# Softmax denominators by a streamed sum in four column groups, and context transposes moved ahead of the turned reciprocals

## The chip, the cores and the metric

The kernel runs on one core of one Trainium2 chip. The metric is the device time of one launch in microseconds. A profiled execution gives a span from the first to the last instruction and a trace of every engine: TensorE (PE, with its weight loads shown as PEld), VectorE (DVE), ScalarE (ACT), GpSimd (POOL) and SyncE (SP), which here issues the transfers of the main loop. Line numbers (L1162) are those of the kernel before.

## The reference

For each of 32 batch elements, with `x` and the context `ctx` of 128 channels or rows by 1024, four blocks follow each other, each adding to `x`. The first is the one that the change touches:

```python
q = einsum('dc,bct->btd', Wq, init) + bq      # init = ctx, d = 64
k = einsum('dc,bct->bdt', Wk, init) + bk
R = einsum('btd,bds->bts', q, k)              # 1024 x 1024 scores
attention = softmax(R, axis=-1)
v = einsum('oc,bct->bto', Wv, layernorm(x)) + bv
x = x + einsum('bts,bsc->bct', attention, v)
...
x = x + ffn(layernorm(x))          # signed weights, scales routed by a softmax
x = x + cross_attention(layernorm(x), ctx)
x = x + low_rank_experts(layernorm(x))
```

All is float32.

## The kernel before

One loop iteration `k` works on three batch elements at once: it *prepares* element `b = k` (loads, queries, keys, values), *attends* for `a = k - 1` (scores, softmax, weighted values of the first block) and runs the *chain* of the three later blocks for `c = k - 2`. The iterations k = 0, 1, 2, 32 and 33 are written out and k = 3 to 31 loop; k = 2 to 31, 30 iterations, hold all three parts. Each engine has one queue, in the order in which its `body` is written, with semaphores between the engines. Nothing is reordered by a planner: what stands behind a wait in a queue waits too.

In the attending part the probabilities of key tile `s` (128 keys by 1024 queries) are made by ScalarE, `prob`. VectorE adds the eight tiles up in `p_sum`, so that the denominator of a query is the sum of its column over the 128 partitions. TensorE makes that sum at s = 7 (L1162): for each of 8 query tiles the tile of `p_sum` is the stationary operand and `ones` (128x8) streams, which leaves the sums with queries on the partitions, in `scores[1]`. Then comes the last `weigh_values` (L1066), which adds the last tile's values into `acc`. VectorE takes the reciprocals, `den_inv` (128 queries by 8 tiles, L921). TensorE turns each column of it, broadcast over 128 columns, into a row that stands on all partitions (eight transposes, L1172, "the turns"). ScalarE copies the two halves into `den_rows` (L715, shown as `prob`, whose memory it is), and VectorE multiplies `acc` by them and adds `x` (`x1_half`, L787 and L788).

The engines' orders around this place, from s = 7 to the end of the iteration, are these:

- TensorE: attended values of the chain (L1151), queries and keys of `b` (L1156), denominators (L1162), last `weigh_values` (L1066), wait for `den_inv`, turns (L1172), eight transposes of `c_in` (L990), wait for `xn_3` normalised, eight transposes of it (L990, shown as `p_sum`), values (L996), the low-rank products (L1193), and first units of the next keys.
- VectorE: p_lo (L878), p_sum (L886), residual of the chain (L913), statistics (L760 to L765), reciprocal (L921), remainders of `q_hl` (L926), `cT_lo` (L930, waits for `cT_hi`), `x1_half`.
- ScalarE: `q_hl` and `k_hh` (L707, L709), `den_rows` (L715, waits for the turns), `cT_hi` (L719, waits for the `c_in` transposes), `xn_3` (L631, `normalize(3)`), `cT_whole` (L726).
- SP: `c_in` is loaded once the feed-forward of the chain and the transposes of the last `c_in` are done (L577, L578), `xn` once the values are done (L580).
- POOL: `rstd` and `shift` of each normalisation (L605, L606).

`c_in` is the context of `b`, and its transposes `cT` become the stationary operand of the next iteration's key products. `scores[0]`, `scores[1]` and `acc` are two PSUM banks each, `shared[0]` and `shared[1]` one each.

Of the kernel before, what the change touches and what calls it, by code (L numbers as in the profile page):

```python
# [24 lines left out]
P = 128  # L25
HALF = 512
# [22 lines left out]
def build(nc, x, ctx_, wq0, bq0, wk0, bk0, wv0, bv0, w_ffn, b_ffn, gate, ics, ocs,  # L49
# [6 lines left out]
    T = D // P  # L56
# [6 lines left out]
    with top:  # L63
        def sb(name, shape, dt=F32, stack=top):
            return stack.enter_context(nc.sbuf_tensor(name, shape, dt))

        def sem(name, stack=top):
            return stack.enter_context(nc.semaphore(name))


        ident = sb("ident", [P, P])
        ones = sb("ones", [P, T])
        minus_half = sb("minus_half", [P, 1])
        wqkT = sb("wqkT", [P, P])
        wvT = sb("wvT", [P, P])
# [308 lines left out]
        with ExitStack() as shared_memory:  # L384
            c_in = sb("c_in", [P, D], F32, shared_memory)
# [18 lines left out]
        p_sum = sb("p_sum", [P, D])  # L404
        x1 = sb("x1", [P, D])
        kw = x1
        kwT = sb("kwT", [P, T, P])
        den_inv = sb("den_inv", [P, T])
        den_rows = prob[0]
        unread = prob[1]  # L410

# [36 lines left out]
        scores = [psum(f"scores{i}", [P, D]) for i in range(2)]  # L448
# [16 lines left out]
        cT_done = sem("cT_done")  # L465
# [6 lines left out]
        scores_done = sem("scores_done")  # L472
        pv_done = sem("pv_done")
        den_done = sem("den_done")
        den_turned = sem("den_turned")
        kwT_done = sem("kwT_done")
        xnT_done = [None] + [sem(f"xnT_done{i}") for i in (1, 2, 3)]
# [28 lines left out]
        den_inv_ready = sem("den_inv_ready")  # L506
# [19 lines left out]
        x3_ready = sem("x3_ready")  # L526
# [15 lines left out]
        def half(h):  # L542
            return slice(h * HALF, (h + 1) * HALF)
# [5 lines left out]
        def nth(per, b, n):  # L549

            if isinstance(b, int):
                return max(0, per * min(b, NB - 1) + n)
            return b * per + n
# [10 lines left out]
        with nc.Block() as block:  # L566
# [182 lines left out]
            def _(dve):  # L749
# [62 lines left out]
                def body(k, prepare, attend, chain):  # L812
                    b, a, c = k, k - 1, k - 2
# [103 lines left out]
                        statistics(dve_chain, 3, c, res)  # L917
                    if attend:
                        dve.wait_ge(den_done, nth(1, a, 1))
                        dve.wait_ge(den_turned, nth(2, a - 1, 2))  # L920
                        nc.vector.reciprocal(den_inv[:, :], scores[1][:, 0:T * T].rearrange("p (t e) -> p t e", t=T)[:, :, 0]  # L921
                                             ).then_inc(den_inv_ready, 1)
                    if prepare:
                        for h in range(2):
                            dve.wait_ge(q_hi_ready, nth(2, b, h + 1))
                            nc.vector.scalar_tensor_tensor(q_hl[DQK:P, half(h)], scores[0][0:DQK, half(h)], bqk_col[0:DQK, :],  # L926
                                                           q_hl[0:DQK, half(h)].bitcast(F32), ALU.add,
                                                           ALU.subtract).then_inc(q_ready, 1)
                        dve.wait_ge(cT_hi_ready, nth(1, b, 1))
                        nc.vector.tensor_tensor(cT_lo[:, :, :].rearrange("p t c -> p (t c)"), shared[0][:, :],  # L930
                                                cT_hi[:, :, :].rearrange("p t c -> p (t c)").bitcast(F32),
                                                ALU.subtract).then_inc(cT_lo_ready, 1)
# [49 lines left out]
            def _(pe):  # L982
                mm = nc.tensor.matmul
                pe.wait_ge(const_made, 4)

                def transposes(h, src, semaphore):

                    for j in range(4):
                        t = 4 * h + j
                        last = nc.tensor.transpose(shared[h][:, j * P:(j + 1) * P], src[:, t * P:(t + 1) * P], ident[:, :])  # L990
                    last.then_inc(semaphore, 1)
# [66 lines left out]
                def weigh_values(a, s):  # L1058
                    if s == 0:
                        pe.wait_ge(kw_ready, nth(2, a, 2))  # L1060
                        pe.wait_ge(v_ready, nth(2, a, 2))
                    pe.wait_ge(p_hi_ready, nth(8, a, s + 1))
                    pe.wait_ge(p_lo_ready, nth(8, a, s + 1))
                    for v, p, first, end in ((v_hi, p_hi, s == 0, False), (v_lo, p_hi, False, False), (v_hi, p_lo, False, s == T - 1)):
                        for h in range(2):
                            last = mm(acc[:, half(h)], v[:, s, :], p[s % 2][:, half(h)], start=first, stop=end)  # L1066
                    last.then_inc(pv_done, 1)

                def body(k, prepare, attend, chain):
                    b, a, c = k, k - 1, k - 2  # L1070
                    for t in range(T):
# [16 lines left out]
                        if chain and t == 5:  # L1088
                            pe.wait_ge(routeT_ready, nth(1, c, 1))
                            pe.wait_ge(r_exp_ready, nth(1, c, 1))  # L1090
                            for h in range(2):
                                for j in range(4):
                                    f = 4 * h + j
                                    last = mm(shared[h][:, j * P:(j + 1) * P], ics3[:, f * P:(f + 1) * P], route3T[:, :],
                                              start=True, stop=True)
# [25 lines left out]
                    for s in range(T):  # L1121
                        if attend and s + 2 < T:
                            key_scores(a, s + 2)
                        if chain and s == 3:
                            pe.wait_ge(normed[2], nth(1, c, 1))
                            for h in range(2):
                                transposes(h, xn_2, xnT_done[2])
                        if chain and s == 4:

                            pe.wait_ge(xnT_a_ready[2], nth(1, c, 1))  # L1130
                            pe.wait_ge(xnT_b_ready[2], nth(1, c, 1))
                            pe.wait_ge(kwT_ready, nth(2, c, 2))
                            pe.wait_ge(key_col_ready, nth(1, c, 1))
                            for f in range(T):
                                mm(shared[0][:, 0:P], xnT[:, f, :], kwT[:, f, :], start=f == 0, stop=False)  # L1135
                            mm(shared[0][:, 0:P], key_col[:, :].to_broadcast([P, P]), ident[:, :], start=False,
                               stop=True).then_inc(sc1_done, 1)
                        if attend and s == 4:
                            transposes(1, kw, kwT_done)
                        if chain and s == 6:  # L1140
                            pe.wait_ge(attn_ready, nth(1, c, 1))
                            pe.wait_ge(kwT_ready, nth(2, a, 1))
                            nc.tensor.transpose(shared[1][:, 0:P], attn[:, :], ident[:, :]).then_inc(attnT_done, 1)
                        if attend and s == 6:
                            transposes(0, kw, kwT_done)
                        if chain and s == 7:
                            pe.wait_ge(attnT_ready, nth(1, c, 1))
                            pe.wait_ge(kwT_ready, nth(2, a, 2))
                            pe.wait_ge(val_loaded, nth(16, c, 16))
                            for h in range(2):  # L1150
                                mm(shared[h][:, :], attnT[:, :], c_val[:, half(h)], start=True, stop=True).then_inc(att_done, 1)  # L1151
                        if prepare and s == 7:
                            pe.wait_ge(c_loaded, nth(16, b, 16))
                            pe.wait_ge(exp_ready, nth(8, a, 7))
                            for h in range(2):
                                mm(scores[0][:, half(h)], wqkT[:, :], c_in[:, half(h)], start=True, stop=True).then_inc(qk_done, 1)  # L1156
                        if attend and s == 7:

                            pe.wait_ge(p_summed, nth(7, a, 7))
                            pe.wait_ge(exp_ready, nth(8, a, 8))  # L1160
                            for t in range(T):
                                last = mm(scores[1][:, t * T:(t + 1) * T], p_sum[:, t * P:(t + 1) * P], ones[:, :], start=True, stop=True)  # L1162
                            last.then_inc(den_done, 1)
                        if attend:
                            weigh_values(a, s)
                    if attend:

                        pe.wait_ge(den_inv_ready, nth(1, a, 1))
                        for h in range(2):
                            for j in range(4):  # L1170
                                t = 4 * h + j
                                last = nc.tensor.transpose(scores[1][:, t * P:(t + 1) * P],  # L1172
                                                           den_inv[:, t:t + 1].to_broadcast([P, P]), ident[:, :])
                            last.then_inc(den_turned, 1)
                    if prepare:
                        for h in range(2):
                            pe.wait_ge(x3_ready, nth(2, c, h + 1))
                            transposes(h, c_in, cT_done)
                    if chain:
                        pe.wait_ge(normed[3], nth(1, c, 1))  # L1180
                        for h in range(2):
# [54 lines left out]
```

## Time and profile before

| | |
|---|---|
| Median of 3 runs | 2358.14 us (2357.36 to 2358.26) |
| Profiled execution, its own time | 2354.89 us |
| Its span | 2353.0 us |
| Mean granted clock of TensorE | 0.982 of full speed |
| TensorE busy | 2198.7 us (93%) |
| VectorE busy | 1874.6 us (80%) |
| ScalarE busy | 1104.3 us (47%) |
| GpSimd busy | 258.9 us (11%) |

The execution's own time is 1.9 us more than its span. The durations of instructions come from the profiled execution; neighbours on one engine overlap a little in it, so a pair's row can show less than twice one's duration. Granted clock 1.00 is 2.4 GHz and 0.50 is 1.2 GHz. A float32 matmul appears as two passes, a transpose as one. The idle time in brackets stands ahead of the row that ends it, with the instruction that released it.

### The profile page before, as it was taken

The page shows a single profiled execution, that of the slowest core. Times are in us where ns is not written, and L with a number is a line of the kernel's source. Part 1 is how long each engine was busy: PE and PEld are TensorE (multiplying, and loading weights), DVE is VectorE, ACT ScalarE, POOL GpSimd, SP SyncE. Part 2 cuts the span into 40 slices and gives each one's busy share as a digit, 9 for nine tenths or more (in the row PEclk, how much of TensorE's full clock was granted, in tenths as well). Part 3 has the DMA queues.
Part 4 walks back from the last instruction along what each step waited for, and adds up shares of the span by engine and source line. Part 5 has one row for each costly group of instructions (what it writes and reads, how often), then busy time and mean ns, then how long its engine had stood idle before and what let it go on. Part 6 is the DMA issues. An engine that isn't in the chain of part 4 may idle for free.

```text
span 2353.0 us, 33856 instructions
## 1 busy us (share of the span) xinstructions
PE 2198.7 (93%) x11102; PEld 1708.4 (73%) x11102; DVE 1874.6 (80%) x3130; ACT 1104.3 (47%) x1593; POOL 258.9 (11%) x296
## 2 busy tenths in 40 slices
PE   1997999999999999999999999999999999999986
PEld 1785777777777777777777777777777777777764
DVE  1436788888888888888888888888888888888873
ACT  2004444555554544555554544555555544555541
POOL 0000111111011111111011111111111111111100
PEclk7999999999999999999999999999999999999996
DMA  8001111111111111111111111111111111111100
GB/s 239 10 1 54 37 54 36 53 53 53 36 53 45 45 53 43 46 53 53 36 53 46 44 53 53 36 53 53 38 51 53 44 45 53 36 53 53 47 16 27
DMA packets 50217, 115.58 MB, mean 49 GB/s; under 512 B 14800, under 2 KB 23248, under 8 KB 50192
## 3 DMA queue, kind: packets, MB, share of 16 engines
q1 hardware_dynamic: 38624, 113.26, 14.5%
q10 hardware_dynamic: 11568, 1.98, 0.5%
q8 instruction: 16, 0.26, 0.0%
q14 instruction: 9, 0.07, 0.0%
HBM read 81.67 MB, written 16.78 MB: 42 GB/s over the span
## 4 chain that ended last, share of the span: by engine, by line
PE 85%; ACT 4%; issue 2%; DVE 2%; DMA 0%; POOL 0%; ACTq 0%; SPq 0%; POOLq 0%; DVEq 0%
PE acc L1066 15%; PE acc L1027 10%; PE shared L1040 5%; PE shared L1041 5%; PE shared L990 5%; PE scores L1010 5%; PE scores L1055 5%; PE scores L1054 5%; PE shared L1151 3%; PE acc L1023 3%; PE acc L1024 3%; PE acc L1025 3%; PE shared L1193 3%; PE shared L1135 3%; PE scores L1162 2%; PE shared L1083 2%
## 5 line engine op out<-in xcount | busy, mean ns | idle before, releaser
L878 DVE TENSOR_TENSOR p_lo<-prob,p_hi 128x1024 fp32r<-128x1024 f32 x256 | 312.3, 1220 | 105.8 <-ACT p_hi L685 88.0
L678 ACT ACTIVATE prob<-scores 128x1024 f32<-128x1024 f32 x256 | 260.5, 1018 | 229.3 <-PE scores L1055 178.1
L771 DVE TENSOR_REDUCE neg_max<-scores 128x1 f32<-128x1024 f32 x256 | 312.2, 1220 | 65.2 <-PE scores L1010 59.8
L605 POOL TENSOR_TENSOR rstd<-var_eps,minus_half 128x1 f32<-128x1 f32 x128 | 126.9, 991 | 1908.4 <-DVE var_eps L765 1908.4
L685 ACT ACTIVATE p_hi<-prob 128x1024 fp32r<-128x1024 f32 x256 | 271.3, 1060 | 42.8 <-PE acc L1066 38.6
L1027 PE MATMUL acc<-m_whole,cT_whole 128*128 128x512 f32 x512 | 255.2, 600 | 0.0
L886 DVE TENSOR_TENSOR p_sum<-p_sum,prob 128x1024 f32<-128x1024 f32 x192 | 233.9, 1218 | 0.0
L1010 PE MATMUL scores<-k_hh,q_hl 128*128 128x512 f32 x512 | 212.7, 496 | 0.0
L1040 PE MATMUL shared<-signT,y_hi 128*128 128x512 f32 x512 | 206.8, 404 | 0.4 <-ACT oscale L667 0.4
L1041 PE MATMUL shared<-signT,y_lo 128*128 128x512 f32 x512 | 203.9, 398 | 0.0
L1054 PE MATMUL scores<-q_hl,k_hh 128*128 128x512 f32 x512 | 200.9, 392 | 1.8 <-DVE q_m L860 1.4
L1055 PE MATMUL scores<-q_m,k_l 128*128 128x512 f32 x512 | 201.7, 394 | 0.0
L1066 PE MATMUL acc<-p_hi,v_hi 128*128 128x512 f32 x512 | 171.4, 416 | 4.2 <-DVE p_lo L878 3.9
L1066 PE MATMUL acc<-p_hi,v_lo 128*128 128x512 f32 x512 | 161.6, 397 | 0.0
L1066 PE MATMUL acc<-p_lo,v_hi 128*128 128x512 f32 x512 | 161.2, 396 | 0.0
L1010 PEld LDWEIGHTS scores<-k_hh,q_hl 128*128 128x128 f32 x512 | 97.2, 190 | 79.1 <-issue 60.9
L990 PE MATMUL shared<-ident,p_sum 128*128 128x128 f32 x512 | 69.7, 280 | 57.6 <-ACT p_sum L631 57.6
L1027 PEld LDWEIGHTS acc<-m_whole,cT_whole 128*128 128x128 f32 x512 | 90.0, 190 | 38.0 <-issue 30.6
L1040 PEld LDWEIGHTS shared<-signT,y_hi 128*128 128x128 f32 x512 | 97.3, 190 | 26.2 <-DVE y_lo L794 0.9
L1054 PEld LDWEIGHTS scores<-q_hl,k_hh 128*128 128x128 f32 x512 | 96.4, 188 | 25.4 <-DVE q_m L860 1.8
L1023 PE MATMUL acc<-m_hi,cT_hi 128*128 128x512 f32 x256 | 109.9, 429 | 4.1 <-DVE cT_lo L930 2.2
L1066 PEld LDWEIGHTS acc<-p_lo,v_hi 128*128 128x128 f32 x512 | 96.4, 188 | 23.6
(215 smaller groups left out, 4354.8 us busy)
## 6 DMA issues: line engine op xcount, KB each, us to landing
c_in<-in_ctx SPq DMA_DIRECT2D x32, 512.0 KB, 3.3
xn<-in_x SPq DMA_DIRECT2D x32, 512.0 KB, 4.1
x<-in_x SPq DMA_DIRECT2D x32, 512.0 KB, 3.3
c_val<-in_ctx SPq DMA_DIRECT2D x32, 512.0 KB, 3.5
out_x<-oscale SPq DMA_DIRECT2D x32, 512.0 KB, 2.9
q_m<-q_hl SPq DMA_DIRECT2D x32, 256.0 KB, 3.1
k_hh<-k_hh SPq DMA_DIRECT2D x32, 256.0 KB, 3.5
wq_nat<-in_L_xattn_Wq SPq DMA_DIRECT2D x4, 1024.0 KB, 10.0
```

The lines of the kernel that those rows point to most:

```text
L678: nc.scalar.activation(prob[s % 2][:, :], scores[s % 2][:, :], ACT.Exp).then_inc(exp_ready, 1)
L685: nc.scalar.activation(p_hi[s % 2][:, :], prob[s % 2][:, :], ACT.Identity).then_inc(p_hi_ready, 1)
L771: nc.vector.tensor_reduce(neg_max[:, t:t + 1], scores[t % 2][:, :], AX_X, ALU.max, negate=True).then_inc(row_max, 1)
L878: nc.vector.tensor_tensor(p_lo[s % 2][:, :], prob[s % 2][:, :], p_hi[s % 2][:, :].bitcast(F32), ALU.subtract).then_inc(p_lo_ready, 1)
L886: nc.vector.tensor_tensor(p_sum[:, :], p_sum[:, :], prob[s % 2][:, :], ALU.add).then_inc(p_summed, 1)
L1010: last = mm(scores[t % 2][:, half(h)], q_hl[:, t * P:(t + 1) * P], k_hh[:, half(h)], start=True, stop=True)
L1027: last = mm(acc[:, half(h)], cT_whole[:, f - TS, :], m_whole[:, f - TS, half(h)], start=f == 0, stop=f == T - 1)
L1040: mm(shared[h][:, :], y_hi[:, f, :], signT[:, f, half(h)], start=f == 0, stop=False)
L1041: last = mm(shared[h][:, :], y_lo[:, f, :], signT[:, f, half(h)], start=False, stop=f == T - 1)
L1054: mm(scores[s % 2][:, half(h)], k_hh[:, s * P:(s + 1) * P], q_hl[:, half(h)], start=True, stop=False)
L1055: last = mm(scores[s % 2][:, half(h)], k_l1[:, s * P:(s + 1) * P], q_m[:, half(h)], start=False, stop=True)
L1066: last = mm(acc[:, half(h)], v[:, s, :], p[s % 2][:, half(h)], start=first, stop=end)
```

## The change

The roles in the denominator sum are swapped: `ones`, now 128x32, is the stationary operand and `p_sum` streams, 256 columns in each of four matmuls, one in each 32-column group of the array. Each writes 32 equal rows of sums, with queries along the free dimension. VectorE copies the 128x256 result to `den_wide`, and TensorE transposes its two halves into `scores[1]`'s second bank, so that the sums stand with queries on partitions again. The reciprocal reads one column of 32. It now stands behind the `q_hl` remainders in VectorE's queue, and the copy stands in its old place. In TensorE's queue the two new transposes stand behind the last `weigh_values`, and the eight transposes of `c_in` stand ahead of the turns instead of behind them. ScalarE's, POOL's and SP's programs are unchanged.

```diff
-        ones = sb("ones", [P, T])
+        ones = sb("ones", [P, 32])
+        den_wide = sb("den_wide", [P, 2 * P])
...
@@ VectorE, at the end of an iteration
                     if attend:
                         dve.wait_ge(den_done, nth(1, a, 1))
-                        dve.wait_ge(den_turned, nth(2, a - 1, 2))
-                        nc.vector.reciprocal(den_inv[:, :], scores[1][:, 0:T * T].rearrange("p (t e) -> p t e", t=T)[:, :, 0]
-                                             ).then_inc(den_inv_ready, 1)
+                        nc.vector.tensor_copy(den_wide[:, :], scores[1][:, 0:2 * P]).then_inc(den_wide_ready, 1)
                     if prepare:
                         for h in range(2):
                             dve.wait_ge(q_hi_ready, nth(2, b, h + 1))
                             nc.vector.scalar_tensor_tensor(q_hl[DQK:P, half(h)], ...
+                    if attend:
+                        dve.wait_ge(den_cols_done, nth(1, a, 1))
+                        dve.wait_ge(den_turned, nth(2, a - 1, 2))
+                        nc.vector.reciprocal(den_inv[:, :].rearrange("p (g j) -> p g j", j=2),
+                                             scores[1][:, half(1)][:, 0:2 * P].rearrange("p (j g r) -> p g j r", j=2, g=4)[:, :, :, 0]
+                                             ).then_inc(den_inv_ready, 1)
+                    if prepare:
                         dve.wait_ge(cT_hi_ready, nth(1, b, 1))
...
@@ TensorE
                             pe.wait_ge(p_summed, nth(7, a, 7))
                             pe.wait_ge(exp_ready, nth(8, a, 8))
-                            for t in range(T):
-                                last = mm(scores[1][:, t * T:(t + 1) * T], p_sum[:, t * P:(t + 1) * P], ones[:, :], start=True, stop=True)
+                            for g in range(4):
+                                last = mm(scores[1][32 * g:32 * g + 32, 0:2 * P], ones[:, :], p_sum[:, g * 2 * P:(g + 1) * 2 * P],
+                                          start=True, stop=True, tile_position=(0, 32 * g))
                             last.then_inc(den_done, 1)
                         if attend:
                             weigh_values(a, s)
+                    if attend:
+                        pe.wait_ge(den_wide_ready, nth(1, a, 1))
+                        for j in range(2):
+                            last = nc.tensor.transpose(scores[1][:, HALF + j * P:HALF + (j + 1) * P],
+                                                       den_wide[:, j * P:(j + 1) * P], ident[:, :])
+                        last.then_inc(den_cols_done, 1)
+                    if prepare:
+                        for h in range(2):
+                            pe.wait_ge(x3_ready, nth(2, c, h + 1))
+                            transposes(h, c_in, cT_done)
                     if attend:
                         pe.wait_ge(den_inv_ready, nth(1, a, 1))
...
                             last.then_inc(den_turned, 1)
-                    if prepare:
-                        for h in range(2):
-                            pe.wait_ge(x3_ready, nth(2, c, h + 1))
-                            transposes(h, c_in, cT_done)
```

## Rows read from the trace of the kernel before

**Rows 1.** The page, part 1: busy time and share of the span of each engine.

```profile
PE 2198.7 (93%) x11102; PEld 1708.4 (73%) x11102; DVE 1874.6 (80%) x3130; ACT 1104.3 (47%) x1593; POOL 258.9 (11%) x296
```

**Rows 2.** Waits: who waited for whom; us in total, times, longest.

```profile
ACT prob L715 <- PE scores L1172: 60.6, 32, 6.5
...
PE shared L990 <- ACT p_sum L631: 57.6, 32, 4.9
```

**Rows 3.** The chain that ended last, steady state; start us, us, what.

```profile
1026.10 1.72 PE scores L1156 x4
1027.81 1.69 PE scores L1162 x16
1029.50 1.49 PE acc L1066 x6
1030.99 0.45 PE scores L1172 x4
...
1032.44 0.60 ACT cT_hi L719
1033.07 1.25 ACT p_sum L631
```

**Rows 4.** Timeline of VectorE; start us, us, instruction, idle before it.

```profile
1024.54 1.22 DVE L878 TENSOR_TENSOR p_lo<-prob,p_hi 128x1024 fp32r<-128x1024 f32 x1 [0.59 <-DVE r_inv L908]
1025.68 1.22 DVE L886 TENSOR_TENSOR p_sum<-p_sum,prob 128x1024 f32<-128x1024 f32 x1
...
1029.89 0.15 DVE L765 TENSOR_TENSOR var_eps<-mean_var,var_eps 128x1 f32<-128x1 f32 x1
1029.95 0.20 DVE L921 RECIPROCAL den_inv<-scores 128x8 f32<-128x8 f32 x1
1030.18 1.40 DVE L926 SCALAR_TENSOR_TENSOR q_hl<-scores,bqk_col,q_hl 64x512 fp32r<-64x512 f32 x2
1033.07 0.69 DVE L930 TENSOR_TENSOR cT_lo<-shared,cT_hi 128x512 fp32r<-128x512 f32 x1 [1.49 <-ACT cT_hi L719]
...
1557.50 0.20 DVE L921 RECIPROCAL den_inv<-scores 128x8 f32<-128x8 f32 x1
```

**Rows 5.** Timeline of TensorE and ScalarE behind the denominators.

```profile
1030.83 1.04 PE L1172 MATMUL scores<-ident,den_inv 128*128 128x128 f32 x8
1031.46 1.09 ACT L715 ACTIVATE prob<-scores 128x512 f32<-128x512 f32 x2 [1.66 <-PE scores L1172]
...
1031.70 1.04 PE L990 MATMUL shared<-ident,c_in 128*128 128x128 f32 x8
...
1034.43 1.09 PE L990 MATMUL shared<-ident,p_sum 128*128 128x128 f32 x8 [1.70 <-ACT p_sum L631]
```

**Rows 6.** Groups by line and shape; busy us, mean ns of one.

```profile
L776 DVE COPY xnT<-shared 128x512 f32<-128x512 f32 x96 | 66.0, 688 | 34.8 <-PE shared L990 34.8
...
L954 DVE TENSOR_TENSOR low<-shared,route 128x128 f32<-128x128 f32 x32 | 9.3, 292 | 1.1
```

**Rows 7.** Timeline of the last attending iteration.

```profile
2282.63 0.20 DVE L921 RECIPROCAL den_inv<-scores 128x8 f32<-128x8 f32 x1
...
2283.58 1.08 ACT L715 ACTIVATE prob<-scores 128x512 f32<-128x512 f32 x2 [6.45 <-PE scores L1172]
```

**Rows 8.** Windows: length, busy of five engines, granted clock, DMA share, GB/s.

```profile
245.64:247.52 1.88, 0.01 (x2) 0.01 (x1) 1.81 (x4) 0.60 (x1) 0.00 (x0) 1.00 0.00 0
...
249.00:252.40 3.40, 3.40 (x9) 2.65 (x8) 2.96 (x7) 1.24 (x1) 2.96 (x3) 0.50 0.00 0
...
2284.00:2285.80 1.80, 0.00 (x0) 0.00 (x0) 1.45 (x2) 1.79 (x3) 0.00 (x0) 1.00 0.00 0
...
2289.90:2292.70 2.80, 0.29 (x2) 0.14 (x1) 1.82 (x10) 0.39 (x2) 0.74 (x2) 1.00 0.00 0
2293.60:2296.90 3.30, 3.30 (x12) 2.32 (x11) 1.38 (x2) 0.84 (x2) 0.33 (x1) 0.50 0.02 5
...
300.00:2276.00 1976.00, 1919.11 (x9775) 1494.46 (x9774) 1696.89 (x2842) 1016.76 (x1468) 242.49 (x268) 1.00 0.14 47
```

More of the change, by code:

```diff
@@ L474, in build @@
         den_done = sem("den_done")
+        den_wide_ready = sem("den_wide_ready")
+        den_cols_done = sem("den_cols_done")
         den_turned = sem("den_turned")
```

## The prediction

> **What bounds the kernel now.** I read the page first, then the waits, then the chain that ended last, then the timeline of one iteration around the edit. The page [rows 1] has TensorE busy for 93% of 2353.0 us and VectorE for 80%. TensorE is the first suspect, but 7% of its time is idle, and the waits say where [rows 2]: ScalarE waits for the turned reciprocals (L715) once in each of 32 iterations, 60.6 us in all, and TensorE waits for ScalarE's normalised rows (L631, `p_sum` as `xn_3`) 57.6 us in 32 waits. The chain [rows 3] shows that the edit sits on exactly this piece. It runs through TensorE's L1156, the denominators L1162, the last `weigh_values` and the first four turns (L1172), then leaves TensorE: ScalarE copies the turned rows (L715 twice), makes `cT_hi` (L719), normalises (L631), and only then do the eight `xn_3` transposes run. So the first four L1172 turns release a ScalarE sequence of fixed length which sets TensorE's next start; behind that TensorE is nearly dense. Iterations repeat at a distance of 65.94 us, from two reciprocals eight iterations apart [rows 4]. What matters is one number: how much earlier or later the turns start.
>
> What holds the turns now? Two things must be there: TensorE's queue must reach them, and `den_inv` must be made. The timeline [rows 4] has the reciprocal at 1029.95, right behind the statistics (L765 at 1029.89), done at 1030.15. The turns start at 1030.83 [rows 5], when the last `weigh_values` is through. TensorE decides, and VectorE is early by about half a microsecond. VectorE has no gap from L878 at 1024.54, its last idle time, until it waits for `cT_hi` for 1.49 us before 1033.07 [rows 4]; so nothing in its queue can start earlier than now.
>
> **The change, part by part.**
>
> *Denominator sums.* Removed are 8 matmuls that ran as 16 passes in 1.69 us [rows 3]. Added are 4 matmuls with 256 columns each, 8 passes if float32 again takes two passes. L1156 streams 512 columns a pass in 1.72/4 = 0.43 us [rows 3], so 256 columns are 0.215 us. If the four column groups run one after another that is 1.72 us, as now; if they overlap fully, 0.43 us, a saving of 1.27 us. No row shows matmuls in column groups. A worse bound: eight turns follow each other in 0.87 us but take 1.04 us with the last one's end [rows 5], a tail of 0.17 us; if each of the 8 passes paid it, they would take 1.4 us more.
>
> *The copy to `den_wide`.* VectorE, 128x256 float32 out of PSUM. A 128x512 copy is 0.69 us (L776), a 128x128 operation 0.29 us (L954) [rows 6]; between them 0.42 us. Bounds 0.29 and 0.69 us.
>
> *The order on VectorE.* Now: statistics, reciprocal 0.20, then the two `q_hl` remainders (L926) 1.40 us. After: statistics, copy 0.42, `q_hl` 1.40, then the reciprocal. It starts at 1029.95 + 0.42 + 1.40 = 1031.77, less about 0.07 by which neighbours overlap (L878 and L886) [rows 4]: 1031.70. That is 1.75 us later, and no TensorE saving moves it, since L765 precedes it all. Its other input, the two transposes, follows the copy (done 1030.37) by 0.22 us of issue plus a tail, done before 1031.4, so it does not wait for them. Queued behind the later reciprocal is `cT_lo`, which waits for `cT_hi` anyway.
>
> *TensorE's way to the turns.* The two new transposes are 2 x 0.87/8 = 0.22 us, the eight of `c_in` 0.87 us [rows 5]. With serial sums TensorE reaches the turns at 1030.83 + 0.03 + 0.22 + 0.87 = 1031.95; with overlapping ones it waits for the copy and gets there at about 1030.42 + 0.22 + 0.87 = 1031.5. The reciprocal ends at 1031.90. So serial or parallel hardly matters: the 1.27 us is taken by VectorE's order.
>
> *How late the turned rows are.* In the last attending iteration `den_inv` was what TensorE waited for, which gives the latency: reciprocal start 2282.63, ScalarE's L715 at 2283.58 [rows 7], 0.95 us. Then L715 starts at 1031.70 + 0.95 = 1032.65 instead of 1031.46 [rows 5]: 1.2 us later. With the copy's bounds, 1.05 to 1.45 us.
>
> *The moved `c_in` transposes.* They cost nothing where they are now: they lie in ScalarE's sequence, and TensorE still waits 1.70 us after them [rows 5]. Moved ahead of the turns they are hidden in VectorE's `q_hl` work, but they also leave the later gap. The sequence from the turns' start to `xn_3` was 1034.43 - 1030.83 = 3.60 us; as `den_inv` now comes last it is 0.75 + 2.97 = 3.72 us (0.95 less the 0.20 of the reciprocal, and L715 to the transposes as now), of which only 1.04 us are turns. TensorE's gap grows from 1.70 to 2.7 us. The `c_in` buffer is free 0.9 us earlier, but SP's next load into it also waits for the feed-forward of the next iteration, and SP's queue issues nothing sooner; `xn` is loaded when `values` are done, which slips with the rest. POOL's shift for L631 is early either way. Nothing downstream can give the 1.2 us back: `cT_hi`, `cT_lo`, `x1` and the values all hang on the same turned rows.
>
> *TensorE's clock.* The granted clock is 1.00 (2.4 GHz) from 300 to 2276 us, across all the gaps of 1.70 us. Outside that stretch it falls to 0.50 (1.2 GHz) after some gaps [rows 8]: after 1.88 us idle (245.64 to 247.52) the stretch from 249.0 to 252.4 is at 0.50; after 2289.90 to 2292.70, with 0.29 us of work in 2.80, the stretch from 2293.6 to 2296.9 is; after 1.80 us idle before 2285.8 it stays at 1.00. The steady gap is just on the good side, and 2.7 us is like the gap of 2290 that led to a fall. A spell lasted 3.3 to 3.4 us in both, costing up to 1.7 us of dense work; some of it lies in the gap itself, so I take 1.5 us. How many gaps are caught isn't readable; I take three in four (22 of 30), bounds none and all. A page of the Trainium skill has this too: "TensorE: Matmul & The Clock Gate", section "Why this matters for your kernels", wants no long idle gaps between bursts of matmuls. The gap length that it names is a little more than this one, so by it the clock would hold and the sum would be 2394 us; by the rows at 245 and 2290 it falls, 2427 us.
>
> **The sum.** 30 iterations (k = 2 to 31) have all three stages: 30 x 1.2 = 36 us. Clock spells 22 x 1.5 = 33 us. The attending iterations at either end lack statistics or `q_hl` work; I set their sum at 0, within 2 us. Together 69 us on the profiled execution's 2354.9 us, 2424 us; the median of the runs lies 3.2 us above it, so 2427 us.
>
> **Rivals.**
>
> *The clock holds.* Only the later reciprocal counts: 2358 + 36 = 2394 us. For it: 30 gaps of 1.70 us and one of 1.80 us passed. Against: a gap of 1.88 us didn't.
>
> *TensorE becomes the bound.* If the column groups run serially and with tails, TensorE arrives after the reciprocal. At the worst price it is 1.4 us more in each of 30 iterations, 42 us on top: 2436 us with a held clock, some 2450 to 2470 us with falls. It decides from 1.72 us upward for the sums. "TensorEngine Tiling (Array Packing)" of the Trainium skill, section "Key Properties", says that changing the tiling mode drains TensorE, which speaks against this change: twice an iteration. With the tail of 0.17 us as price that would be 0.3 us an iteration where the sums are serial, 10 us, or 2437 us; without the rule 2427 us. No row here shows a drain.
>
> *The sums' saving reaches the end (faster).* If TensorE's arrival alone set the turns, overlapping groups would save 1.27 us less the 0.22 us of the new transposes; `c_in` also goes ahead, but fills a gap. 32 x 1.05 = 34 us, 2324 us. It needs `den_inv` by 1030 or so, with VectorE's copy and reciprocal both out of the way; the statistics end at 1030.04 and 1.8 us stand before the reciprocal. I see no way for it unless the queue is not what the trace shows.
>
> *It doesn't matter.* If the ScalarE sequence had 1.2 us of slack elsewhere, time would stay near 2358 us; the 32 waits of TensorE for L631 speak against it.
>
> **How the numbers follow.** Chances: late reciprocal with clock falls 0.68 (its own range 2405 to 2440), clock holds 0.15, TensorE the bound 0.10, no matter 0.04, saving reaches the end 0.03. A measurement of this kernel can tell about 0.2% (5 us) from no change. Range 2389 to 2440: from the held clock with a cheap copy up to falls in every iteration; left out are the dear half of the TensorE case, the two unlikely ones and the tails. Faster 0.03, same 0.04, slower 0.93.
>
> **What would show it.** In the changed profile: the reciprocal starts about 1.8 us behind the statistics, after two L926-like operations; TensorE waits for `den_inv` or arrives level with it; ScalarE's wait before the `den_rows` copies grows by 1.2 us an iteration; the gap before the `xn_3` transposes is near 2.7 us; the granted clock shows spells of 0.50 in the middle of the span. I am wrong if the sums take well over 1.72 us, if the clock row is all 9s, or if the reciprocal isn't late.

## The result, and the profile after

The changed kernel takes 2457.1 us (median of 4 runs, 2454.7 to 2458.3) against 2357.8 us before (4 runs): 1.0423 times as long, interval 1.0405 to 1.0441, or 99 us more. Slower was forecast; 2427 us was too little, and the range ended at 2440 us. The profiled execution has a span of 2456.5 us and a mean granted clock of 0.953 instead of 0.982.

The page, part 1 and the clock row of part 2, answers to [rows 1]:

```profile
PE 2248.1 (92%) x10910; PEld 1719.9 (70%) x10910; DVE 1890.7 (77%) x3162; ACT 1104.5 (45%) x1593; POOL 258.9 (11%) x296
...
PEclk7999999999999999999999999999999999999996
```

TensorE's busy time rose by 49 us although its instructions fell by 192: something made the same matmuls longer. The clock row shows nothing of it. It is still all 9s in the middle, as a digit is the mean of 61 us, so one of the tests that I had named for the forecast was blunt. Windows narrow enough show it, and the waits say where to put them. These answer to [rows 2]:

```profile
ACT prob L718 <- PE scores L1191: 99.8, 32, 7.4
...
PE shared L998 <- ACT p_sum L634: 83.8, 32, 4.9
```

ScalarE's wait for the turns grew from 60.6 to 99.8 us (1.2 us an iteration), TensorE's for the normalised rows from 57.6 to 83.8 us (0.8 us an iteration). One iteration, timeline of VectorE, ScalarE and TensorE, which answers to [rows 4, 5]:

```profile
1065.46 1.88 PE L1164 MATMUL scores<-c_in,wqkT 128*128 128x512 f32 x4
...
1067.27 0.64 PE L1170 MATMUL scores<-p_sum,ones 128*32 128x256 f32 x8
...
1067.84 0.74 PE L1074 MATMUL acc<-p_hi,v_hi 128*128 128x512 f32 x2
...
1069.42 0.15 DVE L768 TENSOR_TENSOR var_eps<-mean_var,var_eps 128x1 f32<-128x1 f32 x1
1069.48 0.42 DVE L923 COPY den_wide<-scores 128x256 f32<-128x256 f32 x1
...
1069.93 1.40 DVE L927 SCALAR_TENSOR_TENSOR q_hl<-scores,bqk_col,q_hl 64x512 fp32r<-64x512 f32 x2
...
1069.95 0.44 PE L1178 MATMUL scores<-ident,den_wide 128*128 128x128 f32 x2 [0.44 <-DVE den_wide L923]
...
1070.23 1.04 PE L998 MATMUL shared<-ident,c_in 128*128 128x128 f32 x8
...
1071.36 0.21 DVE L933 RECIPROCAL den_inv<-scores 128x8 f32<-128x8 f32 x1
...
1071.62 1.09 PE L1191 MATMUL scores<-ident,den_inv 128*128 128x128 f32 x8 [0.36 <-DVE den_inv L933]
1072.31 1.08 ACT L718 ACTIVATE prob<-scores 128x512 f32<-128x512 f32 x2 [2.99 <-PE scores L1191]
...
1075.28 1.97 PE L998 MATMUL shared<-ident,p_sum 128*128 128x128 f32 x8 [2.57 <-ACT p_sum L634]
```

VectorE does what its queue says: statistics over (L768), copy 0.42 us, remainders, reciprocal 1.88 us after the copy's start. TensorE waits 0.44 us for the copy, does the two new and the eight context transposes, waits 0.36 us for the reciprocal, turns, and then waits 2.57 us for ScalarE, where it was 1.70 us before. The last row is the one to stop at: the same eight transposes that took 1.09 us in [rows 5] take 1.97 us. Windows of the same iteration and of another (columns as in [rows 8]):

```profile
300.00:2376.00 2076.00, 1968.44 (x9610) 1505.58 (x9609) 1715.57 (x2876) 1019.93 (x1472) 242.46 (x268) 0.97 0.14 45
...
1072.80:1075.20 2.40, 0.00 (x0) 0.00 (x0) 1.28 (x2) 2.37 (x5) 0.00 (x0) 1.00 0.00 0
1075.30:1078.60 3.30, 3.30 (x16) 3.30 (x17) 1.98 (x3) 0.93 (x2) 0.00 (x0) 0.50 0.00 0
1078.80:1082.20 3.40, 3.40 (x29) 3.27 (x29) 2.60 (x9) 1.33 (x3) 0.74 (x2) 1.00 0.00 0
382.40:389.10 6.70, 5.94 (x28) 5.95 (x29) 5.18 (x12) 2.83 (x5) 0.00 (x0) 0.50 0.00 0
```

Behind the gap the granted clock is 0.50 for 3.4 us, then 1.00 again; I call such a stretch a spell. Read in windows of half a microsecond, each of the 29 iterations between the second reciprocal and the 31st has a spell; in 7 of them it lasts twice as long, as from 382.4 to 389.1. A spell doesn't have to wait for the end of the gap: the trace has them begin between 1.0 us ahead of the `xn_3` transposes and 0.7 us behind their start, and the 7 double ones are the 7 that begin earliest, 0.8 to 1.0 us ahead. The iteration's length follows from two of VectorE's timeline rows:

```profile
310.53 0.21 DVE L933 RECIPROCAL den_inv<-scores 128x8 f32<-128x8 f32 x1
...
2314.78 0.21 DVE L933 RECIPROCAL den_inv<-scores 128x8 f32<-128x8 f32 x1
```

They are 29 iterations apart: (2314.78 - 310.53) / 29 = 69.11 us, where it was 65.94 us: 3.17 us more each. I use this distance below for every kernel, since it leaves out the setup and the tail; for each it is the last full iteration's reciprocal less the first one's, over 29.

### The profile page after: what moved, and what is told of

It is laid out like the page before. It is cut to its first block, busy times and chain, and to the rows that moved or that the text cites. A ratio compares the mean times of both kernels' runs of the same rounds, so it can differ in the third digit from the quotient of the medians.

```text
span 2456.5 us, 33504 instructions
## 1 busy us (share of the span) xinstructions
PE 2248.1 (92%) x10910; PEld 1719.9 (70%) x10910; DVE 1890.7 (77%) x3162; ACT 1104.5 (45%) x1593; POOL 258.9 (11%) x296
## 4 chain that ended last, share of the span: by engine, by line
PE 63%; DVE 15%; issue 9%; ACT 5%; DVEq 0%; DMA 0%; POOL 0%; ACTq 0%; SPq 0%; POOLq 0%
PE acc L1035 9%; PE acc L1074 6%; PE shared L1048 5%; PE shared L1049 5%; PE scores L1018 5%; PE shared L998 5%; DVE p_lo L881 4%; PE scores L1063 4%; PE scores L1062 4%; PE scores L1004 3%; DVE p_sum L889 3%; PE shared L1208 3%; PE acc L1031 2%; PE acc L1032 2%; PE acc L1033 2%
## 5 line engine op out<-in xcount | busy, mean ns | idle before, releaser
L998 PE MATMUL shared<-ident,p_sum 128*128 128x128 f32 x512 | 92.9, 341 | 83.8 <-ACT p_sum L634 83.8
L998 PEld LDWEIGHTS shared<-ident,p_sum 128*128 128x128 f32 x512 | 76.6, 176 | 96.9 <-DVE cT_lo L938 81.4
```

## The experiments

Each ran beside the kernel before, whose medians in these sessions were 2357.0 to 2358.9 us; ratios are to it. A difference of two medians from different sessions can be off by the 2 us between these.

| Kernel | median us | ratio, interval | distance us | spells in 29 |
|---|---|---|---|---|
| changed | 2457.1 | 1.0423 (1.0405 to 1.0441) | 69.11 | 29, 7 of them double |
| changed, gap filled with 7 matmuls | 2399.9 | 1.0170 (1.0153 to 1.0187) | 67.31 | 0 |
| changed, filled with 3 | 2415.7 | 1.0250 (1.0233 to 1.0267) | 67.74 | 8 |
| changed, context transposes back | 2431.0 | 1.0303 (1.0286 to 1.0320) | 68.24 | 18, 10 of them double |
| changed, reciprocal first | 2432.0 | 1.0309 (1.0292 to 1.0326) | 68.27 | 29 |
| the same, filled with 7 | 2382.9 | 1.0109 (1.0092 to 1.0126) | 66.73 | 0 |
| both back | 2370.4 | 1.0050 (1.0033 to 1.0066) | 66.37 | 0 |
| before, context transposes up | 2430.0 | 1.0301 (1.0285 to 1.0316) | 68.26 | 29 |
| before, late reciprocal | 2387.4 | 1.0124 (1.0109 to 1.0139) | 66.92 | 0 |
| copy early | 2358.2 | 0.9999 (0.9990 to 1.0008) | 65.92 | 0 |
| sums hidden | 2334.3 | 0.9897 (0.9882 to 0.9912) | 65.18 | 0 |

### Is it the clock? The gap filled

```diff
@@ TensorE, ahead of the wait for normed[3]
+                    if attend and chain:
+                        pe.wait_ge(den_rows_ready, nth(2, a, 2))
+                        for i in range(7):
+                            mm(scores[1][:, half(0)], signT[:, i, 0:P], signT[:, i, half(1)], start=True, stop=True)
```

The seven results are overwritten by `values` before anything reads them.

> The changed kernel with seven extra matmuls of 512 columns on TensorE (their result is overwritten unread) between the copies of the turned rows and the transposes of the normalised rows, where TensorE now idles. Theory: of the 99 us, about 40 us are the later turns (1.3 us in each of 30 iterations) and the rest is TensorE's clock falling to 0.50 behind the gap of 2.6 us; with the gap filled the granted clock stays near 0.98 and the time is 2395 to 2402 us. Rival (the rest is a cost of the column groups or of the longer queue on TensorE, not the clock): the time stays at 2450 us or more although the gap is filled.

Measured: 2399.9 us. The timeline of TensorE and ScalarE, and the middle of the run in one window:

```profile
1048.14 1.09 PE L1191 MATMUL scores<-ident,den_inv 128*128 128x128 f32 x8 [0.36 <-DVE den_inv L933]
1048.83 1.08 ACT L718 ACTIVATE prob<-scores 128x512 f32<-128x512 f32 x2 [3.00 <-PE scores L1191]
...
1049.96 1.89 PE L1197 MATMUL scores<-signT 128*128 128x512 f32 x7 [0.74 <-ACT prob L718]
...
1051.80 1.09 PE L998 MATMUL shared<-ident,p_sum 128*128 128x128 f32 x8
```

```profile
300.00:2330.00 2030.00, 1973.98 (x9844) 1488.34 (x9843) 1719.16 (x2888) 1020.68 (x1473) 243.53 (x270) 1.00 0.14 46
```

The fill (L1197) occupies 1.89 us of the gap, and the `xn_3` transposes are back at 1.09 us. More work on TensorE made the kernel 57 us faster. The turns are as late as without the fill (TensorE waits 0.36 us for the reciprocal here too), so the distance of 67.31 us gives the delay alone, 67.31 - 65.94 = 1.37 us, and the difference to the unfilled kernel gives the clock, 69.11 - 67.31 = 1.80 us an iteration. The rows account for 1.32 of the 1.37 us: L718 starts 2.89 us behind the statistics' last row (1069.42 to 1072.31), where L715 started 1.57 us behind it (1029.89 to 1031.46, [rows 4, 5]). At most 0.05 us an iteration is left for a cost of the column groups or a longer queue.

With three matmuls in place of seven:

> The changed kernel with three filling matmuls, 0.7 us, in place of seven. Theory: the delay of the turns is the same, 1.37 us an iteration; the clock falls in fewer iterations than in the changed kernel (30 of 30), since more of the stretch is worked: between 2400 us (none) and 2431 us (as many as with the context transposes back). Rival (a gap counts by whether it is broken at all): 2400 us, as with seven.

Measured: 2415.7 us, 8 spells. Timeline of TensorE in an iteration that has one:

```profile
987.50 0.96 PE L1197 MATMUL scores<-signT 128*128 128x512 f32 x3 [0.74 <-ACT prob L718]
...
989.33 1.43 PE L998 MATMUL shared<-ident,p_sum 128*128 128x128 f32 x8 [0.87 <-ACT p_sum L634]
```

A gap is not safe by being broken: with waits of 0.74 and 0.87 us and 0.96 us of matmuls between them, the clock still fell in 8 iterations. The distances inside this run are of two kinds, 67.3 us without a spell and 68.9 us with one, so a single spell costs 1.6 us.

### One step back at a time

Context transposes behind the turns again, the late reciprocal kept:

```diff
@@ TensorE, ahead of the wait for den_inv
-                    if prepare:
-                        for h in range(2):
-                            pe.wait_ge(x3_ready, nth(2, c, h + 1))
-                            transposes(h, c_in, cT_done)
@@ and the same four lines behind the turns, ahead of the wait for normed[3]
```

> The changed kernel with the eight context transposes behind the turns, as before the change; the late reciprocal stays. The turns start as late as in the changed kernel, the last gap shrinks from 2.6 to about 1.7 us, but a gap of about 1.2 us opens ahead of the turns. If only the length of one gap matters to the clock, it holds and the time is about 2398 us. If the idle time close together counts, it goes on falling and the time is 2440 to 2460 us; I expect this one, at 0.6.

Measured: 2431.0 us, below the range that I gave to the likelier case. Timeline of an iteration without a spell:

```profile
1059.36 0.44 PE L1178 MATMUL scores<-ident,den_wide 128*128 128x128 f32 x2 [0.46 <-DVE den_wide L923]
...
1061.04 1.09 PE L1187 MATMUL scores<-ident,den_inv 128*128 128x128 f32 x8 [1.24 <-DVE den_inv L933]
...
1064.69 1.09 PE L998 MATMUL shared<-ident,p_sum 128*128 128x128 f32 x8 [1.70 <-ACT p_sum L634]
```

The last gap is 1.70 us as before the change, but TensorE waits 1.24 us ahead of the turns. 18 of 29 iterations have a spell; those without one are 67.3 us apart, as in the filled kernel, so the delay of the turns is the same. An iteration with a spell, TensorE's rows and one window:

```profile
1128.32 1.42 PE L1187 MATMUL scores<-ident,den_inv 128*128 128x128 f32 x8 [1.24 <-DVE den_inv L933]
...
1132.63 1.96 PE L998 MATMUL shared<-ident,p_sum 128*128 128x128 f32 x8 [1.18 <-ACT p_sum L634]
```

```profile
1129.00:1135.60 6.60, 5.42 (x26) 5.03 (x25) 3.01 (x5) 4.11 (x6) 0.00 (x0) 0.50 0.00 0
```

The clock falls during the turns, ahead of the last gap and not behind it: one of the 18 spells begins with the turns and 17 begin 0.4 to 0.8 us behind their start. In such an iteration the turns and the context transposes run slowly and the last gap is only 1.18 us. So what goes before a fall here is 0.46 and 1.24 us of idle time with two transposes (0.44 us) between them. Neither is as long as the 1.70 us that the kernel before stood through in every iteration.

The reciprocal ahead of the remainders, context transposes still up, and the same kernel filled with the seven matmuls:

```diff
@@ VectorE: the block with the reciprocal moves ahead of the q_hl remainders
                         nc.vector.tensor_copy(den_wide[:, :], scores[1][:, 0:2 * P]).then_inc(den_wide_ready, 1)
+                    if attend:
+                        dve.wait_ge(den_cols_done, nth(1, a, 1))
+                        dve.wait_ge(den_turned, nth(2, a - 1, 2))
+                        nc.vector.reciprocal(...).then_inc(den_inv_ready, 1)
                     if prepare:
                         for h in range(2):
                             dve.wait_ge(q_hi_ready, nth(2, b, h + 1))
```

> The changed kernel with the reciprocal ahead of the two query remainders on VectorE; the context transposes stay ahead of the turns. Theory: the turns are then held by the context transposes, about 0.5 us earlier than in the changed kernel; the gap of 2.6 us is left and the clock still falls in every iteration: 2438 to 2446 us. Rival (VectorE's order was the whole loss): near 2360 us.

> The changed kernel with the reciprocal first on VectorE and the seven filling matmuls in the gap. Theory: the clock holds and only the turns' delay behind the context transposes is left, 0.8 to 0.95 us in 30 iterations: 2382 to 2388 us. The difference to the unfilled kernel's 2432 us is then the price of the clock in it, 1.5 us an iteration, less than in the changed kernel, where some spells last twice as long. Rival (the unfilled kernel loses something other than the clock): above 2400 us.

Measured: 2432.0 and 2382.9 us. The first is a little below its range; the delay is 66.73 - 65.94 = 0.79 us and the clock takes 68.27 - 66.73 = 1.54 us an iteration, all 29 spells being single.

Both moved back, so that only the swapped sums, the copy and the two transposes are left:

> The changed kernel with the reciprocal ahead of the query remainders and the context transposes behind the turns: only the swapped denominator sum, the copy and the two transposes are left of the change. Theory: the turns start 0.3 to 0.4 us later than before the change, as the copy, two transposes and their latencies stand behind the statistics; 2365 to 2372 us if the clock holds, 2400 to 2430 us if the gaps, which add up to more than before, still pull it down. Rival (the saving of 1.0 us on the sums arrives at the end): 2325 to 2340 us.

Measured: 2370.4 us, no spell in the 29 iterations. Timeline:

```profile
1034.09 0.42 DVE L923 COPY den_wide<-scores 128x256 f32<-128x256 f32 x1
...
1034.57 0.44 PE L1178 MATMUL scores<-ident,den_wide 128*128 128x128 f32 x2 [0.48 <-DVE den_wide L923]
...
1035.04 0.21 DVE L927 RECIPROCAL den_inv<-scores 128x8 f32<-128x8 f32 x1 [0.53 <-PE scores L1178]
...
1035.30 1.09 PE L1187 MATMUL scores<-ident,den_inv 128*128 128x128 f32 x8 [0.30 <-DVE den_inv L927]
...
1038.96 1.09 PE L998 MATMUL shared<-ident,p_sum 128*128 128x128 f32 x8 [1.69 <-ACT p_sum L634]
```

Behind the statistics now stand the copy, TensorE's two transposes with VectorE waiting 0.53 us for them, and the reciprocal. The turns come 0.42 us an iteration later than before the change, and of the 1.0 us that TensorE has saved, 0.48 us are waited away ahead of the transposes and 0.30 us ahead of the turns.

### The parts alone, on the kernel before

> The kernel before with one part of the change alone: the eight context transposes ahead of the turns. Theory: they delay the turns by their 0.87 us and leave a gap of about 2.6 us behind the turns; the clock falls in every iteration, as it did with the reciprocal first. 30 x 0.87 us and 30 x 1.45 us of half clock: 2425 to 2435 us, nearly the time of the changed kernel without any of its new matmuls. Rival (the clock falls through the column groups or the missing weight loads of the old sums): about 2385 us.

```diff
@@ TensorE, kernel before: the context transposes move ahead of the wait for den_inv
                         if attend:
                             weigh_values(a, s)
+                    if prepare:
+                        for h in range(2):
+                            pe.wait_ge(x3_ready, nth(2, c, h + 1))
+                            transposes(h, c_in, cT_done)
                     if attend:
                         pe.wait_ge(den_inv_ready, nth(1, a, 1))
```

Measured: 2430.0 us. Timeline of TensorE:

```profile
1057.50 1.03 PE L990 MATMUL shared<-ident,c_in 128*128 128x128 f32 x8
1058.37 1.04 PE L1176 MATMUL scores<-ident,den_inv 128*128 128x128 f32 x8
1061.98 1.97 PE L990 MATMUL shared<-ident,p_sum 128*128 128x128 f32 x8 [2.57 <-ACT p_sum L631]
```

The turns start 0.87 us behind the start of the context transposes, the gap is 2.57 us, the transposes behind it are slow, 1.97 us for eight, and every iteration has its spell. It is TensorE's only wait around this place, and the clock is down 0.4 us before it ends. Eight instructions moved, none added, and the kernel is 72 us slower. The old sums with their many weight loads don't protect the clock, and the clock falls without the column groups.

> The kernel before with its reciprocal behind the two query remainders on VectorE, nothing else. Theory: the reciprocal starts 1.43 us later, the turned rows come 0.87 us later, 26 us in 30 iterations: 2385 us if the clock holds. The idle time moves ahead of the turns (about 0.8 us) beside the last gap of 1.8 us; as that is less together than with the context transposes back in the changed kernel (1.2 and 1.7 us, falls in 18 of 30 iterations), I expect few falls, up to 2400 us. Rival (order on VectorE is hidden): 2359 us.

```diff
@@ VectorE, kernel before: the reciprocal (same lines) moves behind the q_hl remainders
-                    if attend:
-                        dve.wait_ge(den_done, nth(1, a, 1))
-                        ...
                     if prepare:
                         for h in range(2):
                             dve.wait_ge(q_hi_ready, nth(2, b, h + 1))
                             ...
+                    if attend:
+                        dve.wait_ge(den_done, nth(1, a, 1))
+                        ...
```

Measured: 2387.4 us, no spell. Timeline:

```profile
1043.29 0.15 DVE L765 TENSOR_TENSOR var_eps<-mean_var,var_eps 128x1 f32<-128x1 f32 x1
...
1044.90 0.21 DVE L927 RECIPROCAL den_inv<-scores 128x8 f32<-128x8 f32 x1
...
1045.16 1.09 PE L1173 MATMUL scores<-ident,den_inv 128*128 128x128 f32 x8 [0.77 <-DVE den_inv L927]
...
1048.82 1.09 PE L991 MATMUL shared<-ident,p_sum 128*128 128x128 f32 x8 [1.70 <-ACT p_sum L631]
```

VectorE's order alone costs 66.92 - 65.94 = 0.98 us an iteration. The expectation had 0.87: it had the reciprocal start 1.43 us later, and it starts 1.61 us behind the last row of the statistics where it was 0.06, so 1.55 us later.

### Where the saving can arrive

> Swapped sums and context transposes behind the turns, with the copy to the wide tile ahead of VectorE's statistics and the reciprocal right behind them. Theory: the statistics end 0.42 us later than before the change and the reciprocal starts with them; the turns start when TensorE's did before, or up to 0.1 us earlier: 2354 to 2362 us, 9 to 15 us less than with copy and reciprocal both behind the statistics. Rival (the saved 1.0 us on the sums comes through once the copy is early): 2330 to 2340 us.

```diff
@@ VectorE, on top of "both back"
+                    if attend:
+                        dve.wait_ge(den_done, nth(1, a, 1))
+                        nc.vector.tensor_copy(den_wide[:, :], scores[1][:, 0:2 * P]).then_inc(den_wide_ready, 1)
                     if chain:
                         dve.wait_ge(x3_ready, nth(2, c, 2))
                         statistics(dve_chain, 3, c, res)
-                    if attend:
-                        dve.wait_ge(den_done, nth(1, a, 1))
-                        nc.vector.tensor_copy(den_wide[:, :], scores[1][:, 0:2 * P]).then_inc(den_wide_ready, 1)
```

Measured: 2358.2 us, no difference from before the change. Timeline:

```profile
1029.58 0.42 DVE L920 COPY den_wide<-scores 128x256 f32<-128x256 f32 x1 [0.22 <-PE scores L1170]
...
1031.61 0.20 DVE L927 RECIPROCAL den_inv<-scores 128x8 f32<-128x8 f32 x1
...
1031.87 1.09 PE L1187 MATMUL scores<-ident,den_inv 128*128 128x128 f32 x8 [0.55 <-DVE den_inv L927]
```

The copy is off the way, but VectorE's statistics still stand ahead of the reciprocal and decide: TensorE waits for it 0.55 us.

> The same, with the two new transposes ahead of the last two matmuls of the last weighing, and the reciprocal between the two halves of VectorE's statistics. Theory: the reciprocal is then made by about 0.4 us before the end of the weighing or just with it, TensorE decides again, and its saving of 1.04 us on the sums less 0.22 us for the transposes arrives: 0.8 to 0.9 us in 30 iterations, 2330 to 2336 us. Rival (the column groups have a price later, or the clock falls with the shorter run ahead of the gap): 2350 us or more.

```diff
@@ on top of "copy early"; VectorE: statistics() gets a hook, and reciprocals() is passed to it for stage 3
                     nc.vector.bn_stats(stat[i][:, 0:6], src[:, half(0)])
+                    if between is not None:
+                        between()
                     steps.chain(dve, nc.vector.bn_stats(stat[i][:, 6:12], src[:, half(1)]))
@@ TensorE: the two new transposes move into weigh_values, ahead of the last product of the last tile (end is true)
+                        if end:
+                            pe.wait_ge(den_wide_ready, nth(1, a, 1))
+                            for j in range(2):
+                                last = nc.tensor.transpose(scores[1][:, HALF + j * P:HALF + (j + 1) * P],
+                                                           den_wide[:, j * P:(j + 1) * P], ident[:, :])
+                            last.then_inc(den_cols_done, 1)
                         for h in range(2):
                             last = mm(acc[:, half(h)], v[:, s, :], p[s % 2][:, half(h)], start=first, stop=end)
```

Measured: 2334.3 us, 23 us faster than before the change. Timeline:

```profile
1018.17 1.88 PE L1174 MATMUL scores<-c_in,wqkT 128*128 128x512 f32 x4
...
1020.69 0.42 DVE L922 COPY den_wide<-scores 128x256 f32<-128x256 f32 x1 [0.23 <-PE scores L1180]
...
1021.58 0.38 PE L1080 MATMUL scores<-ident,den_wide 128*128 128x128 f32 x2
...
1021.72 0.72 PE L1084 MATMUL acc<-p_lo,v_hi 128*128 128x512 f32 x2
1022.00 0.21 DVE L926 RECIPROCAL den_inv<-scores 128x8 f32<-128x8 f32 x1 [0.29 <-PE scores L1080]
...
1022.27 1.08 PE L1191 MATMUL scores<-ident,den_inv 128*128 128x128 f32 x8
...
1025.92 1.09 PE L1002 MATMUL shared<-ident,p_sum 128*128 128x128 f32 x8 [1.70 <-ACT p_sum L634]
```

TensorE goes from L1174 (L1156 of the kernel before) to the turns in 4.10 us, where it took 4.89 us (1026.10 to 1030.99, [rows 3]), and none of its rows there waits. VectorE waits 0.29 us for the columns. The distance fell by 0.76 us. With the same new matmuls as in the kernel that lost 99 us, TensorE decides again, and its saving comes through.

## Why the prediction was right and wrong

**What bounds the kernel** was read rightly: the turns' start releases a ScalarE sequence of fixed length. From L715 or L718 to the `xn_3` transposes are 2.97 us before and after, and every kernel above moves with the turns.

**The sums.** From the start of the query products to the weighing, TensorE now takes 2.38 us (1065.46 to 1067.84) where it took 3.40 us (1026.10 to 1029.50, [rows 3]); the eight passes took 0.57 us, and 0.10 us more went by ahead of them (1.81 us from the query products, where it was 1.71). The bound was 0.43 us for full overlap, so the four column groups do run side by side. "TensorEngine Tiling (Array Packing)" of the Trainium skill, section "Key Properties", has a drain at each change of mode; the trace leaves at most 0.24 us for both (0.57 + 0.10 - 0.43), and it lay where TensorE waits anyway. The rival in which TensorE becomes the bound needed 1.72 us or more for the sums, so it didn't occur.

**VectorE's order.** Copy 0.42 us, as estimated; the latency of 0.95 us from reciprocal to L718, exact. The reciprocal was 1.94 us behind the statistics' last row instead of 1.81, since it starts only when the remainders are fully done and the overlap of 0.07 us didn't occur; the delay was 1.37 us an iteration, not 1.2. That term was 36 us and measured 41 us (30 x 1.37).

**The gap** of 2.7 us is 2.57 us, as worked out.

**The clock** is the step that failed: not that it falls, but how often and for how long. The prediction's term was "22 x 1.5 = 33 us", with three gaps in four caught and one spell for each. The runs have a spell in 29 of 29 iterations, 22 single and 7 double ones, together 1.80 us an iteration or 54 us in 30. Of the 21 us that the term lacked, 12 are the count (8 more at 1.5 us), and 9 are the double spells: against 67.3 us with the gap filled, iterations with a single spell are 68.6 to 68.9 us apart, 1.3 to 1.6 us more, which bears out the 1.5, and those with a double one are 70.1 us apart, 2.8 us more.

The count was a guess, and the prediction says so; no row stood behind three in four. In the table spells come in none, some or all of 29 iterations, and in all of them in the three kernels whose gap is 2.57 us. The double spell could have been read. The trace of the kernel before has one in its setup, which I didn't show:

```profile
180.90:187.40 6.50, 4.57 (x9) 2.40 (x10) 3.32 (x9) 0.62 (x1) 0.74 (x2) 0.50 0.37 149
```

The range failed with it. Its upper end of 2440 us was a fall in every iteration at 1.5 us each (2358 + 36 + 45 = 2439 us) and had no room for a longer spell. Even my own upper bounds together, a delay of 1.45 us and 1.7 us a spell, give 2358 + 30 x 3.15 = 2453 us, short of 2457.

The two terms, 41 + 54 = 95 us, leave 4 us of the 99. The two profiled executions are 103.5 us apart, not 99: beside the 95 us, 6.0 us lie ahead of the second reciprocal and 2.5 us behind the last one. What makes them I haven't traced; "copy early" has its first reciprocal 5 us later too without being slower.

By the rule on idle gaps in "TensorE: Matmul & The Clock Gate" of the Trainium skill, section "Why this matters for your kernels", this gap was just short enough. The runs disagree: 2.57 us brought a fall in every one of the 29 iterations of three kernels, and in "before, context transposes up" with no other wait near it.

**The other rivals.** That the saving reaches the end was rightly given little, for this order of the queues. "sums hidden" shows it is a matter of that order, and shows a point at which the saving arrives: with the reciprocal ready as the weighing ends.

## What to carry to other kernels

Before counting what an engine saves, ask which engine's queue holds the next hand-over; a saving on the other one turns into waiting, and where the waiting is gathered into one gap, 2.57 us here, it can slow TensorE down as well. Moving work out of a gap to "hide" it costs twice if it delays the hand-over and leaves a gap in which the clock falls: work that stands in an idle stretch on TensorE is useful there. When a small delay costs more than its size, compare like instructions on both sides of the gap (eight transposes, 1.09 us ahead of it and 1.97 us behind) before looking for anything else, and fill the gap with dummy work to price the clock.

## What the runs showed that I had not expected

- Dummy work made a kernel faster: 7 matmuls an iteration, 57 us less.
- Where spells occur they fall into step with the loop. Distances between iterations repeated in a cycle of four in the changed kernel (68.6, 70.1, 68.9, 68.9 us), and two kernels with different delays settled at the same 68.3 us.
- A stretch of idle time counts though it is split: waits of 0.46 and 1.24 us with two transposes between them were followed by a spell in 18 of 29 iterations.
- Neither the longest wait nor their sum orders these kernels. Waits of 0.77 and 1.70 us brought no spell, nor did 0.48, 0.30 and 1.70 us ("both back"), 2.5 us in all; 0.47, 0.36, 0.74 and 0.87 us (filled with 3), 2.4 us in all, brought 8. Where the border lies stays open.
